# Storing a router's selection marks by expert and then by tile

## The reference, cut to what matters

```python
topk_p, topk_i = jax.lax.top_k(probs, K)          # K = 2 of E = 8
one_hot = jax.nn.one_hot(topk_i, E, dtype=x.dtype)
mask = one_hot.sum(1)                             # tokens x experts, 0 or 1
sel = mask.T.astype(bool)
order = jnp.argsort(~sel, axis=1, stable=True)
dispatch = order[:, :capacity]                    # capacity = 320
count = sel.sum(axis=1)
```

## Time and profile before

| | |
|---|---|
| time, median of 3 runs | 156.37 us (156.36 to 156.58) |
| the profiled execution, its own time | 156.25 us |
| its span, first to last instruction | 154.5 us |
| PE busy | 149.5 us, 97% of the span |
| DVE busy | 122.4 us, 79% |
| ACT busy | 109.6 us, 71% |
| POOL busy | 86.7 us, 56% |
| granted clock of TensorE | 1.00 |

### The profile page before, as it was taken

The page is one execution under the profiler, slowest core; times in us unless marked ns, Lnnn a source line. Parts: engine busy times, 40 slices in busy tenths (PEclk is TensorE's granted clock), DMA queues, the critical chain, the costliest instruction groups (busy, mean ns, idle before and its releaser), DMA issues.

```text
span 154.5 us, 3092 instructions
## 1 busy us (share of the span) xinstructions
PE 149.5 (97%) x925; PEld 132.6 (86%) x925; DVE 122.4 (79%) x299; ACT 109.6 (71%) x227; POOL 86.7 (56%) x111
## 2 busy tenths in 40 slices
PE   6999999999999999999999999999999999999992
PEld 6878777888998878998888899999999998788891
DVE  3999969999827999877999677877877866778973
ACT  3369999999495987656964797996875663645860
POOL 7653432767777788777744063689878373460000
PEclk9999999999999999999999999999999999999999
DMA  4999999991110077442239605212321010175562
GB/s 133 300 265 122 185 301 349 339 285 53 52 53 6 8 220 208 122 127 78 68 80 300 196 2 192 63 34 66 100 77 30 28 36 25 30 242 139 204 199 75
DMA packets 26879, 20.82 MB, mean 135 GB/s; under 512 B 2383, under 2 KB 23077, under 8 KB 26864
## 3 DMA queue, kind: packets, MB, share of 16 engines
q1 hardware_dynamic: 24784, 17.86, 43.1%
q0 software_dynamic: 1792, 2.65, 5.4%
q10 hardware_dynamic: 288, 0.14, 0.3%
HBM read 12.46 MB, written 7.92 MB: 132 GB/s over the span
## 4 chain that ended last, share of the span: by engine, by line
PE 84%; DVE 8%; DMA 2%; ACT 1%; issue 1%; POOL 1%; DVEq 0%
PE bank L1259 8%; PE bank L1261 8%; PE bank L1260 8%; PE bank L1388 7%; PE bank L1385 7%; PE bank L1382 7%; PE bank L1344 7%; PE bank L1483 7%; PE bank L1484 7%; PE bank L1485 7%; PE bank L1501 3%; PE bank L1329 2%; DMA acc<-in_L_attn_x_dram 2%; PE bank L1513 1%; PE bank L1357 1%
## 5 line engine op out<-in xcount | busy, mean ns | idle before, releaser
L731 ACT ACTIVATE silu<-bank 128x512 f32<-128x512 f32 (+1 forms) x64 | 33.3, 520 | 27.3 <-PE bank L1388 26.8
L1079 DVE TENSOR_TENSOR bank<-bank,silu 128x320 f32<-128x320 f32 (+1 forms) x56 | 32.7, 584 | 18.4 <-ACT silu L731 11.7
L621 POOL DMA_INDIRECT slots_dram<-row,slot_i x32 | 34.9, 1092 | 10.3 <-issue 9.4
L640 POOL DMA_INDIRECT routed_dram<-eo,xg x24 | 23.3, 970 | 15.5 <-DVE eo L1120 9.9
L1085 DVE TENSOR_TENSOR hid_lo<-bank,hid_hi 128x320 fp32r<-128x320 f32 (+1 forms) x56 | 31.7, 565 | 0.0
L739 ACT CAST hid_hi<-bank 128x320 fp32r<-128x320 f32 (+1 forms) x56 | 27.5, 492 | 0.4 <-DVE bank L1079 0.4
L1382 PE MATMUL bank<-xnT_hi,sw_hi 128*128 128x512 f32 x31 | 13.0, 419 | 0.0
L628 POOL TENSOR_TENSOR ew_lo<-sw_raw,ew_hi 128x1024 fp32r<-128x1024 f32 x3 | 7.2, 2404 | 9.7 <-ACT ew_hi L755 9.7
L1388 PE MATMUL bank<-xnT_hi,sw_lo 128*128 128x512 f32 x31 | 12.3, 398 | 0.0
L1259 PE MATMUL bank<-xnT_hi,sw_hi 128*128 128x512 f32 x31 | 12.3, 397 | 0.0
L1385 PE MATMUL bank<-xnT_lo,sw_hi 128*128 128x512 f32 x31 | 12.3, 396 | 0.0
(11 more groups left out here) (228 smaller groups left out, 387.1 us busy)
## 6 DMA issues: line engine op xcount, KB each, us to landing
sw_raw<-in_L_ffn_rg_dram SPq DMA_DIRECT2D x8, 256.0 KB, 3.0
sw_raw<-in_L_ffn_ru_dram SPq DMA_DIRECT2D x8, 256.0 KB, 3.4
rd_raw<-in_L_ffn_rd_dram SPq DMA_DIRECT2D x8, 256.0 KB, 4.0
routed_dram<-fill SPq DMA_DIRECT2D x1, 2048.0 KB, 11.5
routed<-routed_dram SPq DMA_DIRECT2D x8, 256.0 KB, 4.0
slots_dram<-fill SPq DMA_DIRECT2D x1, 1300.0 KB, 12.3
xg<-slots_dram SPq DMA_DIRECT2D x8, 130.0 KB, 2.7
row<-row SPq DMA_DIRECT2D x1, 1024.0 KB, 8.0
```

Of the source, the lines that this page charges most:

```text
L621: G.indirect_dma_start(slots_dram, bass.IndirectOffsetOnAxis(slot_i[:, k, t:t + 1], 0), row[:, t, 0:RW], None, bounds_check=E * CAP - 1, o ...
L640: G.indirect_dma_start(routed_dram, bass.IndirectOffsetOnAxis(xg[0:n, e % XB, r, 1:2].bitcast(I32), 0), eo[0:n, e % 2, r, :], None, bounds ...
L731: C.activation(silu[:, q % 2, 0:n], gate_bank(q)[:, 0:n], ACT.Silu).then_inc(silu_ready, 1)
L1079: V.tensor_tensor(hid, up[:, 0:n], silu[:, q % 2, 0:n], ALU.mult).then_inc(hid_ready, 1)
```

## The change

The tile `sel` is now stored by expert and then by tile. DVE's sum at L1010 has the same two inputs, read in the same order, and writes its 128 values through a turned view, so that from one value to the next it steps by 16 bf16 values (32 bytes). The two matmuls L1366 and L1368 read the tile as it lies, 128 neighbouring values. No semaphore and no other line is changed.

```diff
-        sel = sb("sel", [P, NT, E], BF16)
+        sel = sb("sel", [P, E, NT], BF16)
...
-                V.tensor_tensor(sel[:, :, :], chosen[:, 0, :, :], chosen[:, 1, :, :], ALU.add
+                V.tensor_tensor(sel[:, :, :].rearrange("p e t -> p t e"), chosen[:, 0, :, :], chosen[:, 1, :, :], ALU.add
                                 ).then_inc(sel_ready, 1)
...
-                s = sel[:, :, :].rearrange("p t e -> p e t")
+                s = sel[:, :, :]
```

## The result

The changed kernel is slower by about 0.2%: a median of 156.75 us over 22 runs (156.42 to 157.26) against 156.37 over 22 runs of the kernel before (156.19 to 156.66). The ratio is 1.0023, with a 95% interval of 1.0016 to 1.0031. Three more measurements of the same pair gave 1.0016 (1.0006 to 1.0026), 1.0028 (1.0013 to 1.0042) and 1.0022 (1.0010 to 1.0034). The forecast was 156.37, no change that can be measured, with a range that ended at 156.67.

What follows compares the result with a forecast made beforehand. PE held 84% of the chain, but DVE's list was late up to `scores(0)`. The profiled 156.25 us, + 0 for the covered write, + 0 for the reads, gave 156.37 on the median's level; range 156.15 to 156.67.

Steps and rivals of the forecast that it cites:

- the price of the write: Extra time of DVE's stepped write at L1010: taken as 0, with 91 and 182 ns as dearer values.
- the sign of being wrong: L1010 taking over 0.70 us in the changed kernel's profile, one of three signs named against the prediction.
- the write is dearer than its cover: Rival: DVE's write costs more than POOL hides; 156.45 us at p = 1.42, 156.78 at p = 4; slower had chance 0.04.
- 128 p - 100 ns: Movement of the end if DVE's write costs p ns more per value and 0.10 us is hidden.
- The point from which it was to decide: p = 3.2 ns a value: 0.41 us more on DVE leaves 0.31 on the chain, enough to measure.
- The cover: POOL's L597, ending at 27.85 us, holds L1016 and so hides up to 0.10 us of a dearer DVE write.
- The matmuls: PE's L1366 and L1368, read without a step, fall from 387 and 386 to 219 to 225 ns; worth 0.
- PE's saving of 0.32: L1366 to L1368 end about 0.32 us earlier, paying for `ranks` starting 0.09 or 0.18 later; counting fully: chance 0.03.
- One for one: Whatever exceeds the 0.10 us of cover moves L1016, the chain behind it, `scores(0)` and the end equally.

Runs made afterwards that it cites:

- e3: The changed kernel with the marks stored as f32 and the matmuls reading the upper half of each as bf16; 156.42 us, ratio 1.0001.
- e13: The kernel before with an extra DVE sum of 256 neighbouring f32 values between `sel` and `hid_s`; 156.73 us, ratio 1.0020.
- e4: The changed kernel's layout, with the turn on DVE's two f32 inputs and the write in one piece; 156.53 us, ratio 1.0007.
- e15: The kernel before with only the matmuls changed: marks read in one piece, results written turned to PSUM; 156.37 us, ratio 1.0001.
- e7: The changed kernel with `y_lo(0)` taken ahead of the slot sums on DVE; 157.59 us, ratio 1.0075.
- e17: The kernel before with L1368 made twice, so PE's down products begin later and DVE is as before; 156.29 us, ratio 1.0008.
- e18: The kernel before with an extra DVE sum of 256 f32 values behind `hid_s`, delaying L1016 but not PE's down products; 156.57 us, ratio 1.0019.
- e2: The changed kernel's stepped write, marks 16 bytes apart by tile and 256 by expert, with matmuls still reading with a step; 156.61 us, ratio 1.0009.
- e12: The kernel before with each bf16 mark 16 bytes from the next, layout order kept; 156.53 us in a single run.
- e9: The kernel before measured against itself, nothing changed; 156.45 us, ratio 1.0000.
- e11: The kernel before with each bf16 mark in a 4-byte word of its own, layout order kept; 156.32 us in a single run.
- e14: The kernel before with one stepped bf16 write into an unread tile, in a wait of DVE at 42 us; 156.30 us, ratio 0.9992.

## Why the prediction was wrong, step by step

**The step that failed is the price of the write.** The prediction took 0 for the stepped write, by L910, and 182 ns as its upper end, twice the stepped read of L1032. It measured 413 ns, and at 704 ns `sel` passed the 0.70 us that the prediction itself had named as the sign of being wrong. Both rows were of 4-byte values, and the write has 2-byte values; at 4 bytes the bound would have been right, as e3's 86 ns show against the 91 that L1032 gave. Of L910's 16 values nothing larger could be told: at 0.67 ns a value they would show 11 ns, and the row showed none of it, yet 128 such values in e3 did pay. The "SBUF Cachelines" section of the Trainium skill's page "Advanced Engine Details and Errata" warned of this write; the prediction gave that warning the price of a read, and took 0. The formula in the section on the TRN2 errata of the Trainium skill's page "VectorE: DVE Perf Modes", element count plus 151 cycles, has no term for a step; it still gives 291 ns for the stepped `sel`, which took 704.

**The rival that came in was "the write is dearer than its cover".** Its formula, 128 p - 100 ns, gives 0.31 us at the measured p = 3.23, so 156.68 us, and the median was 156.75. That this is so near is in part luck: the formula counts the write's whole 413 ns, of which only 0.32 us reached `hid_s`'s end, and the trace shows 0.22 us at L1016 and 0.14 at `scores(0)` where it has 0.31. The point from which it was to decide, p = 3.2, is just where the chip stands. It had a chance of 0.04, because the rows were of the wrong width.

**The cover was right.** POOL's L597 ended at 27.84, 0.10 us of `hid_s`'s 0.32 were hidden, and 0.22 moved L1016; e13 gives the same without the write. That POOL would be slowed by what DVE reads at that time (e4) was not seen.

**The matmuls were right.** 230 ns for a forecast of 219 to 225, and worth nothing (e15). That PE's saving of 0.32 would pay for a later start did not hold, since the start moved 0.41, but PE's list was not the path (e7, e17).

**"One for one" was right in kind and not settled in size.** L1016 is 0.22 us late. In the traces 0.14 to 0.16 of it reach `scores(0)`. Some 0.06 come back at L1036. Timelines of DVE and POOL there, of the kernel before and then of the changed kernel:

```profile
31.23 0.25 DVE L1036 SCALAR_TENSOR_TENSOR slot_i<-over,slot_f 128x32 int32<-128x32 f32 x1
31.22 0.23 POOL L588 TENSOR_TENSOR row<-top_w,shares 128x16 f32<-128x16 f32 x1
31.40 0.23 POOL L589 TENSOR_TENSOR row<-top_w,shares 128x16 f32<-128x16 f32 x1
```

```profile
31.43 0.19 DVE L1036 SCALAR_TENSOR_TENSOR slot_i<-over,slot_f 128x32 int32<-128x32 f32 x1
31.24 0.24 POOL L588 TENSOR_TENSOR row<-top_w,shares 128x16 f32<-128x16 f32 x1
31.44 0.27 POOL L589 TENSOR_TENSOR row<-top_w,shares 128x16 f32<-128x16 f32 x1
```

It starts 0.20 us late and ends 0.14 late. In every trace in which L1036 took 0.25 us, POOL's L588 (here or under a shifted line number) had begun 0.01 to 0.02 us before it. In those that are late by 0.23 us at L1016 it begins near the end of L588 and 0.01 before L589, takes 0.19, and it is L589 that is longer. So the late list misses a POOL instruction that it met before; no run moved POOL alone to show it. In e4, whose L1036 still met L588, the whole 0.11 us reached `scores(0)`.

In the runs 0.19 to 0.43 us arrive, 0.36 in e13 and 0.27 in e18, which delay DVE by the same amount. As far as these runs can tell, the rest beyond the traces goes with DVE's delay and not with the write. Where it arises stays open. A hint lies behind `scores(0)`: from there to the end of the span the median was 121.60 us in the eight traces with this delay of DVE (the changed kernel's four, e2, e12, e13, e18) and 121.53 in eight without it (the kernel before, e3, e4, e9, e11, e14, e15, e17), but each group spreads over 0.24 us or more.

## What to carry to other kernels

Ask of a layout that is turned for its reader who pays for the turn, and whether that one is on the path: here PE, with time to spare, had its two reads of 387 ns cut to 230, and DVE, with only 0.10 us of cover, paid 413 ns. If a tile of 2-byte marks must be turned, turn it on a 4-byte type (86 ns here, without effect on the time) or leave the step to the engine that waits. Bound a cost by rows of the same width and not only of the same step, and where a chain changes its path after an edit, look at when the old path was ready: rows that overlap can hide the wait for it, and an edit that delays one list alone decides.

## What the runs showed of the hardware that was not expected

- A sum of 128 values on DVE took 291 ns with bf16 outputs side by side, 305 with 4 bytes from one to the next, 696 to 704 with 32, 725 with 16 (e12) and 723 with 256 (e2); with f32 outputs 64 bytes apart it took 377.
- The dear write does not stop DVE from taking in the next instruction: that one started 0.34 us after it, not 0.70, and ran 0.20 us longer itself (0.88 for 0.68). The loss of the pair, 0.32, is less than the 0.41 of its first row.
- Two f32 inputs of a DVE sum with a step of 32 bytes went with a POOL instruction of 0.36 us beside it that took 0.26 otherwise (e4); a stepped f32 output did not (e3).
- The DVE instruction L1036 took 0.25 us where a POOL instruction had begun 0.01 to 0.02 us before it, and 0.19 where none had begun within 0.1 us before it.
- A matmul with 128 columns and a step of 64 bytes in its PSUM output took 283 ns, against 230 without (e15).
